# Attention with eight PSUM banks: scores in three banks, maxima and jobs in a ring of four

## The reference, cut to what matters

```python
q, k, v = jnp.split(x @ Wqkv, 3, axis=-1)              # 16 heads of 16 features
q = q * cos + rotate_half(q) * sin                     # self-attention only; k likewise
attn = jax.nn.softmax(jnp.einsum('bhtd,bhsd->bhts', q, k) * scale, axis=-1)
out = jnp.einsum('bhts,bhsd->bhtd', attn, v)
x = layernorm(x + out @ Wout)
```

## Time and profile before

| | us |
|---|---|
| median of 3 runs | 1545.46 |
| lowest, highest | 1537.97, 1546.08 |
| the profiled execution, whole | 1557.11 |
| its span in the trace | 1555.4 |
| of it: loop (five FIRST and five SECOND halves), 271.1 to 904.9 | 633.8 |
| of it: halves with scores ahead of and behind the loop | 206.9 and 192.0 |

### The profile page before, as it was taken

How to read it: one execution, slowest core, us unless ns; L and a number is a source line. 1 busy time by engine, 2 the same in 40 slices (tenths; PEclk the granted TensorE clock), 3 DMA queues, 4 the chain that set the end, 5 groups by cost and what they waited for, 6 DMA issues and landing times. The chain is left out here.

```text
span 1555.4 us, 27690 instructions
## 1 busy us (share of the span) xinstructions
PE 1402.5 (90%) x8424; PEld 845.7 (54%) x8424; DVE 1115.6 (72%) x2282; ACT 907.3 (58%) x1702; POOL 439.5 (28%) x411
## 2 busy tenths in 40 slices
PE   2889899999999999999999998999588889999984
PEld 2424354544435444454444443443277779999974
DVE  3788388888789888889879878757256544555466
ACT  3276547656666666666766676646245445555544
POOL 4211131032014013105103201100125544666654
PEclk8699889989999999999999999979789889999997
DMA  3451622433343343244243334140135435778762
GB/s 124 126 159 35 188 81 77 138 103 120 105 136 121 102 128 125 67 148 121 77 139 109 117 101 137 42 110 2 37 136 185 155 105 109 154 131 165 150 178 82
DMA packets 108089, 179.85 MB, mean 116 GB/s; under 512 B 20288, under 2 KB 65984, under 8 KB 103872
## 3 DMA queue, kind: packets, MB, share of 16 engines
q1 hardware_dynamic: 93376, 159.11, 33.1%
q0 software_dynamic: 14592, 19.41, 7.1%
HBM read 98.09 MB, written 79.30 MB: 114 GB/s over the span
## 5 line engine op out<-in xcount | busy, mean ns | idle before, releaser
L618 DVE TENSOR_REDUCE nm<-ps_max 128x1 f32<-128x512 f32 x1024 | 640.6, 681 | 107.0 <-PE ps_max L810 106.7
L576 ACT ACTIVATE prob<-ps_sc 128x512 f32<-128x512 f32 x1024 | 557.9, 597 | 267.5 <-PE ps_sc L824 262.9
L810 PE MATMUL ps_max<-qk 48*128 48x512 f32 x1024 | 442.2, 494 | 31.4 <-DVE nm L618 17.1
L824 PE MATMUL ps_sc<-qk 50*128 50x512 f32 x1024 | 406.6, 466 | 34.0 <-ACT prob L576 33.7
L824 PEld LDWEIGHTS ps_sc<-qk 50*128 50x128 f32 x1024 | 166.5, 189 | 346.5 <-ACT prob L576 294.4
L841 PE MATMUL ps_out<-prob,va 128*32 128x512 f32 x2048 | 279.7, 619 | 1.4 <-ACT prob L576 1.2
L810 PEld LDWEIGHTS ps_max<-qk 48*128 48x128 f32 x1024 | 177.6, 192 | 90.7 <-DVE nm L618 68.7
L1573 PE MATMUL ps_gu<-x2f,we 128*128 128x256 f32 (+1 forms) x1344 | 222.1, 320 | 4.6 <-ACT sg L1238 2.4
L1573 PEld LDWEIGHTS ps_gu<-x2f,we 128*128 128x128 f32 x1344 | 189.2, 191 | 21.9 <-DVE h L1464 3.1
L458 POOL TENSOR_TENSOR rstd<-mv,eps 128x2 f32<-128x2 f32 x32 | 6.4, 201 | 621.7 <-DVE mv L687 621.7
L1573 PE MATMUL ps_dn<-we,hf 128*128 128x256 f32 x864 | 122.6, 298 | 11.3 <-DVE totals L1547 10.5
(11 more groups left out here) (145 smaller groups left out, 1467.3 us busy)
## 6 DMA issues: line engine op xcount, KB each, us to landing
qk<-hbm_self SPq DMA_DIRECT2D x384, 64.0 KB, 2.4
qk<-hbm_cross SPq DMA_DIRECT2D x384, 64.0 KB, 2.3
hbm_self<-stage SPq DMA_DIRECT2D x16, 1024.0 KB, 4.0
hbm_cross<-stage SPq DMA_DIRECT2D x16, 1024.0 KB, 4.2
slots_x<-zeros SPq DMA_DIRECT2D x8, 1360.0 KB, 5.9
xs<-slots_x SPq DMA_DIRECT2D x40, 272.0 KB
weraw<-w_moe SPq DMA_DIRECT2D x11, 768.0 KB
x2in<-x SPq DMA_DIRECT2D x16, 512.0 KB, 4.3
```

The source lines that it names most:

```text
L576: nc.scalar.activation(prob[:, s % 2, j, :], ps_sc[:, (HG * s + j) % NSC, :], ACT.Exp, scale=HD ** -0.5).then_inc(exp_done[a], 1)
L618: nc.vector.tensor_reduce(nm[:, g % 2, r:r + 1], ps_max[:, n % NMX, :], axis=AX.X, op=ALU.max, negate=True).then_inc(max_done[a], 1)
L810: nc.tensor.matmul(ps_max[:, n % NMX, :], qk[rows, 0, pair, P * c:P * c + P], qk[rows, 1, pair, :], start=True, stop=True).then_inc(smax_d ...
L824: nc.tensor.matmul(ps_sc[:, n % NSC, :], qk[rows, 1, h // 2, P * c:P * c + P], qk[rows, 0, h // 2, :], start=True, stop=True).then_inc(st_ ...
```

## The change

The banks are divided anew: three for scores (`NSC`), one for `ps_out`, and four (`RING`) that maxima and jobs share in the order in which PE issues them. Score n waits for exponential n-3, and the first scores of an instance wait for the exponential that last used their bank (`score_bank` keeps the rotation going over the instances). Each maximum and each job takes the next bank of the ring and waits for the reader of whatever had it before, that is the tile four takes earlier, be it a maximum or a job. Each half has 84 takes with its jobs; in FIRST two turns are skipped at step 13 (`SKIP`), where maximum 16 of the next instance thus waits for the reduction two before it instead of three. The instructions that compute stand in the same order on each engine as before; only banks and waits differ, and PE has four more rows of register and loop work.

```diff
-NSC, NMX = 2, 3
+NSC, RING = 3, 4
+SKIP_AT, SKIP = 13, 2
...
+    def ring_users(self):
+        users = []
+        for s in range(self.steps):
+            turn = self.maxima(s)
+            if self.name == "first" and s == SKIP_AT:
+                users += [None] * SKIP
+            for j in range(HG):
+                if turn:
+                    users.append(("max", *turn[j]))
+                users += [t for t in self.table.get(s, []) if is_job(t[0]) and j == job_at(t[0])]
+        return users
...
+def score_bank(a, n):
+
+    return (n + a) % NSC
...
         ps_sc = ctx.enter_context(nc.psum_tensor("ps_sc", [P, NSC, T], F32))
-        ps_max = ctx.enter_context(nc.psum_tensor("ps_max", [P, NMX, T], F32))
+        ps_ring = ctx.enter_context(nc.psum_tensor("ps_ring", [P, RING, T], F32))
         ps_out = ctx.enter_context(nc.psum_tensor("ps_out", [P, T], F32))
-        ps_job = ctx.enter_context(nc.psum_tensor("ps_job", [P, 2, T], F32))
...
+            def free(user):
+
+                if user and user[0] == "max":
+                    (a, b), n = user[1:]
+                    pe.wait_ge(max_done[a], b * NMAX + n + 1)
+                elif user:
+                    kind, n, b = user
+                    pe.wait_ge(read[kind], upto(kind, b, n))
...
-                if n >= NMX:
-                    pe.wait_ge(max_done[a], b * NMAX + n - NMX + 1)
-                elif before:
-                    pe.wait_ge(max_done[before[0]], before[1] * NMAX + NMAX)
-                nc.tensor.matmul(ps_max[:, n % NMX, :], qk[rows, 0, pair, P * c:P * c + P], qk[rows, 1, pair, :],
+                nc.tensor.matmul(bank(slot), qk[rows, 0, pair, P * c:P * c + P], qk[rows, 1, pair, :],
...
-                    pe.wait_ge(exp_done[before[0]], before[1] * NMAX + NMAX)
+                    m = max(m for m in range(NMAX) if score_bank(before[0], m) == score_bank(a, n))
+                    pe.wait_ge(exp_done[before[0]], before[1] * NMAX + m + 1)
...
+                def take(user, key):
+
+                    at = slots[key]
+                    free(owners[at])
+                    owners[at] = user
+                    return at
```

More of the change, by code:

```diff
@@ L109 @@
     table: dict
-    former: list
+    before: object
     cur: tuple = None
@@ L151, in before_loop @@
     lead.loads, lead.clear = {0: [("x", 0)]}, None
-    own = second(-1)
+    own = second(-1, lead)
     own.loads = {8: [("x", 1)]}
@@ L171, in behind_loop @@
     table = {s: [t for t in row if exists(t[2])] for s, row in close_behind("nm1", B - 2, B - 1).items()}
-    late = Half("close", table, [], c6, c7, s7, (CROSS, B - 3), s7, start=START,
+    seventh = first(B - 1, second(B - 2))
+    late = Half("close", table, seventh, c6, c7, s7, (CROSS, B - 3), s7, start=START,
                 loads={2: [("c", B - 1)]}, cross={10: (B - 1, 0), 13: (B - 1, 1)},
                 stacks={0: (c6, s7, 3), 12: (c7, c6, 0), 13: (c7, c6, 1)})
[L175 to L184, removed]
+    gap = Half("gap", gap_of(B - 1), late, None, c7, c6, s7, c6, steps=GAP, start=START - STEPS, stacks={0: (c7, c6, 2)})
+    last = Half("last", shifted(LAST, B - 2), gap, c7, None, c6, s7, None, stacks={0: (c7, c6, 3)}, result={14: B - 2})
+    post = Half("post", shifted(TASKS[FIRST], B + 1), last, None, None, c7, c6, c7, result={14: B - 1})
+    return [seventh, late, gap, last, post]
 def upto(kind, b, n):
@@ L275, in every_period, with bank @@
             with eng.Fori(2, B - 1) as k:
-                half(first(k))
-                half(second(k))
+                half(first(k, second(k - 1)))
+                half(second(k, first(k)))
             for h in behind_loop():
                 half(h)
[L281 to L299, removed]
+        def bank(slot):
+            return ps_ring[:, slot, :]
         def wait_done(eng, s, kind, b, n):
@@ L593, in _, with split_lo @@
             dve.wait_ge(consts_dma, 48)
-            def split_lo(kind, b, n, out, high, bias=None, value=None):
-                value = bank(kind, n, b) if value is None else value
+            def split_lo(kind, b, n, out, high, value, bias=None):
                 dve.wait_ge(hi_done[kind], upto(kind, b, n))
@@ L604, in split_lo, with maximum @@
                 ins.then_inc(read[kind], 1)
-            def maximum(inst, before, n):
+            def maximum(inst, before, n, slot):
                 (a, b), g = inst, n // (HG * TT)
@@ L699, in half @@
             def half(h):
+                slots = h.slots
                 for s in range(h.steps):
-                    turn = maxima_of(h, s)
-                    for kind, n, b in behind(h, s):
+                    turn = h.maxima(s)
+                    for kind, n, b, of in h.behind(s):
                         if kind not in ("nm0", "nm1"):
-                            task(kind, n, b)
+                            task(kind, n, b, of.get((kind, n)))
                     for j in range(HG):
@@ L848, in half @@
                     pe.wait_ge(w_ready, 5)
+                owners, slots = (h.before.owners() if h.before else [None] * RING), h.slots
+                def take(user, key):
[3 more added lines that the diff above has]
+                    return at
                 for s in range(h.steps):
-                    ahead = [(inst, h.prv if inst is h.cur else h.cur or h.prv, n) for inst, n in maxima_of(h, s)]
+                    turn = h.maxima(s)
                     for j in range(HG):
```

158 lines of the change are left out of this document (86 added, 72 removed).

## The result

| | before | changed |
|---|---|---|
| median, us | 1544.05 (4 runs) | 1497.67 (4 runs) |
| lowest, highest | 1537.97, 1546.08 | 1484.86, 1503.56 |
| ratio to before, 95% interval | | 0.9684 (0.9635 to 0.9733) |
| the profiled execution, its span | 1557.11, 1555.4 | 1484.86, 1483.1 |
| loop in the trace | 633.8 | 605.3 |

The account below looks back on a forecast made before the run. DVE, busy 107.7 of a 126.3 us period, and PE, estimated at 108, wait on each other. Terms 2.4 + 1.8 + 1.5 + 0.5 - 0.4 give 5.8 us a period, 46.7 overall: 1545.5 to 1499 us, range 1483 to 1530.

Parts of the forecast that it names:

- The sum: All terms together: 5.8 us off the loop's 126.3 us period, 46.7 us off the kernel, to a median of 1499 us.
- One sign of being wrong: In the loop: the forecast is wrong if the clock there falls below 1.00, its full level of 2.4 GHz.
- Three score banks: Steps without a job: a shorter chain through the scores, 2.66 us instead of 3.17, saving 2.4 us a period.
- The ring behind `w0` and `w1`: Four steps with these large jobs: the job starts 0.44 us earlier in each, 1.8 us a period.
- The other 12 large jobs: Large jobs other than `w0` and `w1`: 1.5 us a period in all, between 0 and 5.3.
- The start of an instance: First maximum no longer waits for all 64 former reductions: 0.25 us at each of two starts, 0.5 a period.
- What the ring adds: New waits at step 1 of both halves and step 13 of FIRST: 0.4 us a period lost, between 0 and 1.3.
- Outside the loop: Halves before and after the loop: 5.8 for another period, 3.5, 4.4 and 4 us, 17.7 us gained in all.
- The ring did not take half back: Rival: sharing banks between maxima and jobs takes back much of the gain, 1522 us; chance 0.19 for 1514 to 1533.
- No change: Rival: DVE sets the pace and PE's waits only move, time within 8 us of 1545; chance 0.09.
- Slower: Rival: DVE reads `ck`, `cq`, `nt`, `xt` banks over 0.23 us later, stopping PE at maxima; 1570 us, chance 0.06.
- The rule by weight loads: Skill's measure of PE: weight loads busy 28.99 of 64.9 us, 45%, so more headroom than the estimated 108 us a period.

Follow-up runs that it names:

- the ring alone: Changed kernel with two score banks again, keeping the ring of four, one bank unused: 1542.11 us, ratio 0.9859 to before.
- the wait on POOL: Changed kernel with POOL's `x1b` additions waiting until DVE finishes the cross-attention's four layernorm instructions: 1499.57 us, ratio 0.9588 to before.
- the kernel with the split layernorm: Changed kernel with the cross-attention's layernorm on DVE split, two instructions ahead of step 12's maxima, two ahead of step 13's: 1516.44 us, ratio 0.9799.

## Why the prediction was right, point by point

**The sum.** Predicted 1499 us, measured 1497.67. The mechanism was right, but that the number is right to 1.3 us is luck. The period was to go from 126.3 to 120.5 us and does where the clock stays full (61.4 + 59.1); with the falls the mean is 121.1. The loop gave 28.5 us of 29, but it took 616.4 and 606.4 us in the two other profiles of this kernel, which would be 17.4 and 27.4. The profiled execution was to take 1510 us and took 1484.86; 20 of those 25 us are the mixture of experts. And the terms came out less evenly.

**The clock.** One sign of being wrong came true: the clock in the loop is below 1.00 (0.97 in three FIRST halves). It was not at its full level in the whole loop of the kernel before either, as the prediction read it: the earlier trace rows has an 8 in the ninth slice, and the loop's first FIRST half there is

```profile
271.14:338.22 67.08, 64.17 (x357) 30.13 (x356) 52.93 (x96) 42.34 (x81) 7.07 (x9) 0.92 0.41 130
```

The other four took 64.8 to 65.0 us at 1.00, 2.2 us less than this one.

**Three score banks**, predicted 2.4 a period: 2.9 by the difference of the ring alone and both. The chain of exponential, head outputs, third score and two exponentials was right to 0.03 us (2.69 and 2.67 for 2.66).

**The ring behind `w0` and `w1`**, predicted 4 x 0.44 = 1.8: this term failed. By the distances between the steps' first scores, over four periods, step 10 of FIRST gave 0.44, but the others gave nothing: step 8 of SECOND 0.0, step 9 of SECOND 0.17 longer, step 9 of FIRST 0.11 longer, 0.15 in all. I read one of four places and multiplied. In two of the others there was no wait to remove: before, `w0` followed the fourth score by 0.40 us in step 8 of SECOND and `w1` by 0.33 in step 9 of FIRST (691.92 to 692.25), against 1.03 in step 10. Step 8 of SECOND there:

```profile
749.58 0.40 PE L824 MATMUL ps_sc<-qk 50*128 50x512 f32 x1
749.98 1.69 PE L727 MATMUL ps_job<-w,cf 128*128 128x256 f32 x12
```

And step 9 of both halves has a `nm`, which now takes a bank of the ring. In FIRST the transpose stands 0.19 us for a reduction and `w1` 0.10, where neither stood before; in SECOND the fourth maximum still waits, and `w0` comes 1.10 us behind the fourth score instead of 0.95.

**The other 12 large jobs**, predicted 1.5 between 0 and 5.3: 1.9 in all (FIRST 0, 2, 3, 4 gave 0.47, 0.29, 0.23, 0.23 and SECOND 10 gave 0.42, among others; SECOND 5 and 15 lost 0.17 and 0.11). The ring alone has the same two sums, 0.1 and 1.9. The ring as a whole, 1.8 + 1.5 + 0.5 - 0.4 = 3.4 predicted, gave 2.9, and the score bank 2.9 for 2.4: two errors of 0.5 that cancel in the period, which is luck.

**The start of an instance**, predicted 0.5: 0.3, in one of the two places.

**What the ring adds.** Step 1 is 0.17 longer in both halves, 0.34 for the 0.2 predicted. The skip at step 13 was put at 0.2 and moving it changed nothing. Step 13 grew by 1.1 us, but that is no loss by itself: steps 11 to 13 of FIRST together took 10.73 us before, 10.73 with the ring alone and 10.71 with the change. DVE sets the pace there, as the prediction said, and PE, which now gains 1.15 us in steps 11 and 12, stands it off at DVE's block. What the prediction left out is that the clock could fall behind such a stand, and that the block itself could be shortened: with the wait on POOL the three steps take 9.03. The reader of `ck` does not hold the third maximum, as the slack of 0.23 us had said: no wait of PE for `ck`, `cq` or `nt` readers reaches 1 us a period.

**Outside the loop**, predicted 17.7. own0 gave 4.8 for 3.5, the FIRST and SECOND there 4.9 for 5.8. The half last was to give 4.4; by the windows shown it gave 1.8, but these end at its fourth last score. Up to its last score it took 54.2 us before and 54.0 after. Its steps came right at 2.67, but only those without jobs and at full clock; the last two ran at half clock (0.50 from 1040 us on) and took 3.8 and 4.1. The closing halves gave 6.5 and 6.1 where I had 2 each. Most of it is in their last stretch, from the last step's first score over the gap to the next half. The window of it in the first closing half, of before and of the changed kernel:

```profile
185.70:208.60 22.90, 21.31 (x75) 11.26 (x76) 15.79 (x29) 4.74 (x10) 2.53 (x2) 0.72 0.22 55
```

```profile
178.80:196.10 17.30, 16.29 (x77) 8.14 (x74) 15.26 (x27) 5.02 (x10) 2.53 (x2) 0.98 0.23 57
```

The same work, but for a few instructions at the edges, runs at a clock of 0.98 instead of 0.72 and takes 5.6 us less. In the two other profiles of the changed kernel this stretch took 19.9 us at 0.84 and 21.5 at 0.73, so most of that gain belongs to the one execution; in the second closing half it came each time (20.3 us before, 15.9 to 16.0 after). The prediction counted waits only and left the clock out. It came out on the good side here, and on the bad side behind step 13.

**The rivals.** The ring did not take half back. "No change" did not come true: the third score bank gave 2.9 us a period, where PE's wait was for ACT. The case of double-buffering without gain (the Trainium skill, "TensorE: Matmul & The Clock Gate", section "HAM oscillation — how this bites in real kernels") was of a matmul kernel that had been rearranged around its waits for DMA, and the runs here don't follow it. "Slower" rested on the readers of `ck`, which fit. But slower was near in another way: with two banks for maxima, or a ring of three, the same eight banks cost 7.4 and 3.2%. DVE idled 18.6 us of a period before and 13.2 of one after (61.58 + 59.09 less 52.95 + 54.55). Steps without a job behind run-ahead now take 2.24 us, PE's own work of 2.3, so PE has no headroom left there. The rule by weight loads (the Trainium skill, "Perfetto Trace Analysis", section "Identifying the Most-Contended Engine") would see some: their share is 27.60 of 61.58 us, still 45%.

## What to carry to other kernels

Where buffers of two kinds are freed by the same engine in the order of issue, a shared ring does with fewer what separate pools need more for; spend the buffer saved where another engine holds the chain, and check the neighbouring divisions, since one bank moved the wrong way cost 3 to 7% here. When a wait is read at one place, follow it at each place before multiplying. When one step grows, add up its neighbours before calling it a loss. And when two elementwise engines run side by side on SBUF, look at the median of the same instruction elsewhere: if it is twice as long, one may be holding up the other, and one wait on the engine with time to spare can give it back.

## What the runs showed of the hardware

**POOL holds up DVE.** A layernorm instruction from SBUF to SBUF takes 407 ns alone, 816 beside POOL's additions of 256 columns, and beside POOL's one subtraction of 1024 columns, which itself takes 2.36 us, up to 2555. That is the longest in the kernel with the split layernorm:

```profile
L730 DVE TENSOR_SCALAR res<-res,mv,rstd x32: 380/404/2555, 306.6 to 1099.5; 128x256 f32<-128x256 f32 x32
```

Four of DVE's reductions out of PSUM take 2.47 us beside POOL's additions (from 563.71 there) and 2.48 without them. DVE's instruction ends 0.15 us behind POOL's in each such pair of the split kernel and of the change (563.05 behind 562.90, 552.87 behind 552.72), so the trace looks as if DVE were held for the whole of POOL's instruction. The Trainium skill says so, in "SBUF — State Buffer", section "SBUF: two separate sides": the port pair shared by VectorE and GpSimd goes to whichever starts first, for the whole instruction, and the other blocks; VectorE takes the pair in its two-port modes or, against a GpSimd operation that reads SBUF, with two SBUF inputs. DVE's three durations agree with it. The other direction is hardly seen: POOL's additions take 772 ns at the median beside DVE and 727 behind it. In which mode DVE ran, no run shows.

**The clock falls behind a stand of PE, but not behind each.** Step 13's stand of 1.6 us was followed by half clock in three of the changed kernel's five iterations in one profile and not in the other two, and in three profiles of that kernel FIRST took 61.3 to 67.0 us with the clock from 1.00 to 0.90. In the kernel before, where PE's idle at that place is 1.0 us instead of 1.2, it was followed by half clock in one iteration of five. With the wait on POOL, where the longest idle of PE around step 13 is 0.46 us, no fall came in any of the five. Why one stand brings it and the next doesn't was not settled.

**The mixture of experts varies by itself.** From the last score to the end, with the same 2726 matmuls, it took 456.6 us (before), 436.5, 440.1 and 455.8 (changed) and 455.6 (changed, with the wait on POOL). The kernel before took 1544 to 1564 us at the median in the several sets of runs, so kernels of different sets are compared by their ratios only. What sets the time of that part was not tried.
